# Adding each expert's output rows to token rows in DRAM inside the expert loop, in place of 64 gathers at the end

## The reference

```python
top_scores, top_idx = jax.lax.top_k(masked, K)          # K = 4 experts of 32 for each token
gates = jax.nn.softmax(top_scores, axis=-1)
capacity = max(1, int(N / E * K * CAP_FACTOR))          # 2048 / 32 * 4 * 1.25 = 320
pos = jnp.cumsum(onehot, axis=0)[jnp.arange(N * K), flat_e] - 1
keep = pos < capacity
buf = jnp.zeros((E + 1, capacity, d), xf.dtype).at[e_s, p_s].set(xf[tok])[:E]
h = jax.nn.silu(jnp.einsum('ecd,edh->ech', buf, wg)) * jnp.einsum('ecd,edh->ech', buf, wu)
out_e = jnp.einsum('ech,ehd->ecd', h, wd)
gathered = out_e[flat_e, jnp.minimum(pos, capacity - 1)]
contrib = gathered * (flat_g * keep.astype(xf.dtype))[:, None]
routed = jnp.zeros_like(xf).at[tok].add(contrib)
return (shared + routed).reshape(b, s, d)
```

## Time and profile before

| | |
|---|---|
| median of three runs | 1864.75 us |
| the profiled execution: own time | 1868.67 us |
| the profiled execution: span of its records | 1867.0 us |
| PE busy | 1544.0 us (83%) |
| DVE busy | 1014.4 us (54%) |
| ACT busy | 798.5 us (43%) |
| POOL busy | 887.1 us (48%) |
| mean granted TensorE clock | 0.931 of full speed |
| DMA traffic | 118.25 MB |

### The profile page before, as it was taken

One profiled execution on the slowest core, in us unless ns is written; L12 is line 12 of the kernel. 1 busy time (PEld: TensorE's weight loads), 2 busy tenths in 40 slices (PEclk: granted clock), 3 DMA queues, 4 the chain that ended last, 5 costly groups with the idle time before them and its releaser, 6 DMA issues.

```text
span 1867.0 us, 25548 instructions
## 1 busy us (share of the span) xinstructions
PE 1544.0 (83%) x7946; PEld 1085.8 (58%) x7946; DVE 1014.4 (54%) x1423; ACT 798.5 (43%) x1543; POOL 887.1 (48%) x775
## 2 busy tenths in 40 slices
PE   2799999999999999999999996441999999999800
PEld 2455555655555555455555554331789999999800
DVE  5456556556555565655655555710366666666533
ACT  2345344444444544445444444200256666666500
POOL 4356657666665675766666572175000101101175
PEclk8899999999999999999999997575999999999955
DMA  9000000000000000000000001022055555555237
GB/s 305 13 16 18 1 21 13 0 21 12 7 14 12 12 8 12 12 8 12 12 10 11 12 1 68 1 102 78 8 185 188 173 164 184 172 169 184 69 104 121
DMA packets 82412, 118.25 MB, mean 63 GB/s; under 512 B 7940, under 2 KB 56775, under 8 KB 82375
## 3 DMA queue, kind: packets, MB, share of 16 engines
q1 hardware_dynamic: 72647, 90.52, 15.6%
q0 software_dynamic: 9728, 27.28, 5.3%
HBM read 77.29 MB, written 31.46 MB: 58 GB/s over the span
## 4 chain that ended last, share of the span: by engine, by line
PE 60%; issue 13%; POOL 12%; DVE 7%; ACT 4%; another core or an unknown queue 1%; DMA 1%; POOLq 0%; DVEq 0%; ACTq 0%; SPq 0%
PE ps_o L720 9%; PE ps_t L634 9%; PE ps_m L634 7%; POOL arena L548 7%; PE ps_st L634 7%; PE ps_m L685 6%; PE ps_st L705 4%; PE ps_o L816 4%; PE ps_m L816 4%; PE ps_t L740 3%; PE ps_st L709 3%; POOL arena L598 3%; ACT arena L1301 2%; POOL arena L553 2%; PE ps_t L834 2%
## 5 line engine op out<-in xcount | busy, mean ns | idle before, releaser
L548 POOL TENSOR_TENSOR arena<-arena 128x512 f32<-128x512 f32 (+1 forms) x512 | 655.9, 1282 | 395.8 <-ACT arena L1301 368.3
L1301 ACT ACTIVATE arena<-ps_st 128x512 f32<-128x512 f32 (+1 forms) x576 | 326.0, 595 | 453.4 <-PE ps_st L709 442.0
L1002 DVE TENSOR_REDUCE arena_r<-ps_m 128x1 fp32r<-128x1101 f32 x256 | 332.1, 1297 | 306.1 <-PE ps_m L685 305.8
L705 PE MATMUL ps_st<-arena_r 128*128 128x512 f32 (+1 forms) x576 | 263.0, 457 | 23.1 <-ACT arena L1301 23.0
L720 PE MATMUL ps_o<-arena 128*64 128x512 f32 (+1 forms) x1152 | 268.4, 601 | 0.0
L582 POOL DMA_DIRECT2D y_slots<-arena x32 | 23.2, 726 | 437.1 <-ACT arena L1382 343.8
L709 PE MATMUL ps_st<-arena_r 68*128 68x512 f32 (+2 forms) x576 | 228.8, 397 | 0.9 <-DVE arena_r L1009 0.9
L634 PE MATMUL ps_m<-arena_r 128*128 128x320 f32 (+1 forms) x864 | 162.9, 324 | 68.9 <-issue 44.5
L685 PE MATMUL ps_m<-arena_r 128*128 128x512 f32 (+1 forms) x768 | 193.2, 360 | 5.4 <-DVE arena_r L1002 5.4
L685 PEld LDWEIGHTS ps_m<-arena_r 128*128 128x128 f32 x768 | 137.6, 191 | 91.0 <-issue 44.6
L634 PEld LDWEIGHTS ps_m<-arena_r 128*128 128x128 f32 x864 | 137.2, 191 | 75.9 <-issue 50.8
(11 more groups left out here) (144 smaller groups left out, 1899.8 us busy)
## 6 DMA issues: line engine op xcount, KB each, us to landing
arena<-in_L_ffn_wg_dram SPq DMA_DIRECT2D x32, 512.0 KB, 3.6
arena<-in_L_ffn_wu_dram SPq DMA_DIRECT2D x32, 512.0 KB, 4.7
arena<-in_L_ffn_wd_dram SPq DMA_DIRECT2D x32, 512.0 KB, 6.4
x_slots<-zeros SPq DMA_DIRECT2D x1, 10240.0 KB
arena_r<-arena_r SPq DMA_DIRECT2D x32, 275.2 KB, 3.6
arena<-x_slots SPq DMA_DIRECT2D x32, 256.0 KB, 2.7
y_slots<-arena POOLq DMA_DIRECT2D x32, 256.0 KB, 5.5
x_sb<-in_x_dram SPq DMA_DIRECT2D x2, 1024.0 KB, 7.3
```

What stands on the lines that cost most here:

```text
L548: pool.tensor_tensor(acc, probsT[0:rows, h, 0, :] if kt == 1 else acc, probsT[0:rows, h, kt, :], ALU.add).then_inc(added, 1)
L705: pe.matmul(ps_st[0:rows, n % 2, :], k1[b][h][:, r], q1[h][:, c:c + 512], start=True, stop=False)
L1002: dve.tensor_reduce(neg[h][:, c:c + 1], scores_m[:, 0:KEYS], AX.X, ALU.max, negate=True)\
L1301: act.activation(probsT[0:rows, h, kt, :], ps_st[0:rows, n % 2, :], ACT.Exp)\
```

## The change

A row of the slot table becomes 272 numbers in place of 256. Behind the 256 of the token stand the token's id (`TOK`), its four gates (`GATES`) and its four expert numbers (`IDS`). Before the expert loop SP writes `x_sb`, which then holds x plus attention plus shared part, into a DRAM table `acc_rows`. In each window DVE converts the ids to integers and finds the gate of each slot by comparing the four expert numbers with the number of the current expert (`slot_gates`); ACT multiplies by that gate as it copies the product out; and POOL issues three indirect DMAs that add the rows to `acc_rows` at their ids. Empty slots carry the ids of 320 spare rows behind the tokens, with gate 0. `y_slots`, the 64 gathers and the 64 multiply-adds of DVE are gone, and the output is a copy of `acc_rows`, DRAM to DRAM.

```diff
-    YRING = 8
+    RW = D + 16
+    TOK, GATES, IDS = D, D + 1, D + 1 + TOPK
...
-            sp.dma_start(xslots[0:SLOTS, :].rearrange("(p n) d -> p n d", p=P),
-                         zeros[:, :].unsqueeze(1).broadcast_to([P, SLOTS // P, D])).then_inc(init_out, 16)
+            spare = xslots[0:SLOTS, :].rearrange("(e j p) d -> j p e d", e=E, p=FP)
+            for j in range(FJ):
+                sp.dma_start(acc[NTOK + j * FP:NTOK + (j + 1) * FP, :], fill[:, j, 0:D]).then_inc(init_out, 16)
+                sp.dma_start(spare[j], fill[:, j, :].unsqueeze(1).broadcast_to([FP, E, RW])).then_inc(init_out, 16)
...
+            for c in range(NCHUNK):
+                for i in (2, 3):
+                    job_done(sp, J_SHARED + i, c * 2)
+                sp.dma_start(acc[c * 512:(c + 1) * 512, :].rearrange("(t p) d -> p t d", p=P),
+                             x_sb[:, c * 4:c * 4 + 4, :]).then_inc(acc_in, 16)
             sp.wait_ge(xslots_out, 16 * NT * TOPK)
 
             def feed(par, turn, weights):
                 e = turn * 2 + par
 
                 sp.wait_ge(job_ready[1], (J_EXPERT // 2 - 2 + 1) + e)
+                sp.wait_ge(ids_done, e * 2 + 2)
                 sp.dma_start(xg[par][:, 0:CTL - 1, :],
...
+            sp.wait_ge(add_out, 16 * CTL * E)
             for b in range(B):
-                sp.wait_ge(summed, (b + 1) * QT_N)
-                sp.dma_start(out[b].rearrange("(t p) d -> p t d", p=P), x_sb[:, b * QT_N:(b + 1) * QT_N, :])\
-                  .then_inc(final_out, 16)
+                sp.dma_start(out[b], acc[b * S:(b + 1) * S, :]).then_inc(final_out, 16)
...
+            pool.wait_ge(init_out, 32 * FJ)
             attend(BEFORE, -1)
...
-            def store(par, turn):
+            pool.wait_ge(acc_in, 16 * NCHUNK)
+
+            def add(par, turn):
                 e = turn * 2 + par
                 pool.wait_ge(ysb_ready, e * CTL + CTL + 2)
                 pool.sem_inc(pool_step, 1)
-                pool.dma_start(yslots[bass.ds(e * CAP, (CTL - 1) * P), :].rearrange("(c p) d -> p c d", p=P),
-                               y_sb[par][:, 0:CTL - 1, :]).then_inc(ystore_out, 16)
...
-                pool.wait_ge(ystore_out, e * 32 + 32)
+                for c, (_, rows) in enumerate(CAP_TILES):
+                    pool.indirect_dma_start(
+                        out=acc[:, :], in_=y_sb[par][0:rows, c, :], in_offset=None, compute_op=ALU.add,
+                        out_offset=bass.IndirectOffsetOnAxis(ap=ids[0:rows, par, c:c + 1].bitcast(U32), axis=0))\
+                        .then_inc(add_out, 16)
+                pool.wait_ge(add_out, (e + 1) * 16 * CTL)
                 pool.sem_inc(ysb_free, 1)
...
+            dve.sem_inc(ids_done, 4)
...
+            def slot_gates(par, turn):
+
+                e = turn * 2 + par
+                dve.wait_ge(rows_in[par], turn * 32 + 32)
+                dve.wait_ge(ysb_free, e + 1)
+                dve.tensor_copy(ids[:, par, 0:CTL], xg[par][:, :, TOK]).then_inc(ids_done, 1)
+                dve.scalar_tensor_tensor(picks[:, :, :], xg[par][:, :, IDS:IDS + TOPK], iota_e[:, bass.ds(e, 1)],
+                                         xg[par][:, :, GATES:GATES + TOPK], ALU.is_equal, ALU.mult)\
+                   .then_inc(picked_up, 1)
+                dve.wait_ge(picked_up, e + 1)
+                dve.tensor_reduce(slot_gate[:, par, :], picks[:, :, :], AX.X, ALU.add).then_inc(ids_done, 1)
...
                        (lambda ht: ht < 2 and weights_lo(par, n + ht, ht)) if more else None)
+                slot_gates(par, turn)
                 if more:
                     rows_lo((par + 1) % 2, turn + par)
...
-                    act.activation(y_sb[par][0:rows, c, :], ey_bank[(par * CTL + c) % 2][0:rows, 0:D], ACT.Copy)\
+                    act.activation(y_sb[par][0:rows, c, :], ey_bank[(par * CTL + c) % 2][0:rows, 0:D], ACT.Copy,
+                                   scale=slot_gate[0:rows, par, c:c + 1])\
                        .then_inc(ysb_ready, 1)
...
                 act.wait_ge(ysb_free, turn * 2 + par + 1)
+                act.wait_ge(ids_done, (turn * 2 + par) * 2 + 6)
```

More of the change, by code:

```diff
@@ L191, in xattn_moe @@
     WPIECES = 4
[L193 to L194 removed]
+    xslots = nc.dram_tensor("x_slots", [SLOTS + NTOK * TOPK, RW], F32, kind="Internal").ap()
+    acc = nc.dram_tensor("acc_rows", [NTOK + CAP, D], F32, kind="Internal").ap()
     with ExitStack() as stack:
@@ L254, in xattn_moe @@
         w_raw = [carve(3 * W) for _ in range(2)]
-        xg, y_sb = ([carve(CTL * D, "p (c n) -> p c n", c=CTL) for _ in range(2)] for _ in range(2))
-        carve = carver(arena, 6 * W + NT * D)
+        xg, y_sb = ([carve(CTL * n, "p (c n) -> p c n", c=CTL) for _ in range(2)] for n in (RW, D))
+        carve = carver(arena, 6 * W + NT * RW)
         silu, hid32 = ([carve(512) for _ in range(2)] for _ in range(2))
@@ L280, in xattn_moe @@
         ones = sb("ones", [P, P])
-        zeros = sb("zeros", [P, D])
+        FP = 64
+        FJ = CAP // FP
+        assert FJ * FP == CAP
+        fill = arena[0:FP, R_SUM:R_SUM + FJ * RW].rearrange("p (j d) -> p j d", j=FJ)
         gb = sb("gb", [P, 4, DT])
@@ L328, in xattn_moe @@
         rows_in = [sem(f"rows_in{i}") for i in range(2)]
-        ystore_out = sem("ystore_out")
-        yg_in = [sem(f"yg_in{i}") for i in range(YRING)]
+        acc_in, add_out = sem("acc_in"), sem("add_out")
+        ids_done, picked_up = sem("ids_done"), sem("picked_up")
         copies_in = [sem(f"copies_in{i}") for i in range(B)]
@@ L359, in xattn_moe @@
         hid_hi_done, hid_done = sem("hid_hi_done"), sem("hid_done")
-        ey_ready, ysb_ready, ysb_free, summed = (sem(n) for n in ("ey_ready", "ysb_ready", "ysb_free", "summed"))
+        ey_ready, ysb_ready, ysb_free = (sem(n) for n in ("ey_ready", "ysb_ready", "ysb_free"))
         def job_in(ev, turn, off=0):
@@ L496, in _ @@
             seq = Chain(pool, pool_seq)
-            seq.done(pool.memset(zeros[:, :], 0.0))
+            seq.done(pool.memset(fill[:, :, :], 0.0))
             seq.done(pool.memset(ident[:, :], 0.0))
@@ L508, in _ @@
             seq.done(pool.iota(iota_e[:, :], pattern=[[1, E]], base=0, channel_multiplier=0,
+                               allow_small_or_imprecise_dtypes=True))
+            seq.done(pool.iota(fill[:, :, TOK], pattern=[[FP, FJ]], base=NTOK, channel_multiplier=1,
                                allow_small_or_imprecise_dtypes=True))
@@ L581, in store @@
                 pool.sem_inc(pool_step, 1)
-                pool.dma_start(yslots[bass.ds(e * CAP, (CTL - 1) * P), :].rearrange("(c p) d -> p c d", p=P),
-                               y_sb[par][:, 0:CTL - 1, :]).then_inc(ystore_out, 16)
-                lo, rows = CAP_TILES[-1]
-                pool.dma_start(yslots[bass.ds(e * CAP + lo, rows), :], y_sb[par][0:rows, CTL - 1, :])\
-                    .then_inc(ystore_out, 16)
-                pool.wait_ge(ystore_out, e * 32 + 32)
+                for c, (_, rows) in enumerate(CAP_TILES):
[4 more added lines that the diff above has]
+                pool.wait_ge(add_out, (e + 1) * 16 * CTL)
                 pool.sem_inc(ysb_free, 1)
             with pool.Fori(0, E // 2) as i:
[L591 to L601, removed]
+                add(0, i)
+                add(1, i)
         @block.tensor
@@ L1143, in _ @@
             seq.done(dve.tensor_scalar(keep[:, :, :], posk[:, :, :], float(CAP), None, ALU.is_lt))
+            seq.done(dve.tensor_copy(h_row[:, :, IDS:IDS + TOPK], topf[:, :, :]))
+            seq.done(dve.tensor_scalar(h_row[:, :, TOK], dropslot[:, :, 0], -float(SLOTS), 1.0 / TOPK, ALU.add, ALU.mult))
+            seq.wait()
             seq.done(dve.tensor_scalar(topf[:, :, :], topf[:, :, :], float(CAP), None, ALU.mult))
@@ L1154, in _ @@
             seq.wait()
[L1155 to L1158, removed]
+            seq.done(dve.tensor_copy(h_row[:, :, GATES:GATES + TOPK], gate[:, :, :]))
             seq.wait()
@@ L1214, in _ @@
             expert(1, E // 2 - 1, False)
[L1216 to L1222, removed]
         @block.scalar
```

18 lines of the change are left out of this document (10 added, 8 removed).

## The result

The changed kernel takes 1902.89 us (median of 4 runs, 1899.92 to 1905.66) against 1866.12 for the kernel before (4 runs, 1864.67 to 1868.23): 1.0196 times as long, 95% interval 1.0176 to 1.0216, so 36.8 us slower. The profiled execution took 1899.92 us with a span of 1898.0, which is 31.0 us more span than before. (The profiled executions are the fastest of the changed kernel and the slowest of the kernel before, so they lie closer together than the medians.)

A forecast was written before the change was run, and what follows sets the result against it. PE was taken to bound the expert loop, at 12.83 us per expert. Entry 2.1 plus loop 131.1 minus tail 78.6 gave +54.6 us, so 1864.75 became 1919 us, range 1860 to 1990.

The forecast's parts named there:

- The deciding step: Expert loop: SP's new wait for slot_gates(e-2) holds back the weight loads, making a longer loop; 131.1 us more over 30 windows.
- 1. gates to first weight issue: Expert loop, SP: release, two row loads and registers between the end of slot_gates and the first weight issue; 1.4 us.
- 2. issue to last landing: Expert loop, weight DMA: first weight issue to last landing, with the adds running beside it; 7.8 us, bounds 6.8 and 8.8.
- 3. landing to gates, full clock: Expert loop: from landed weights through ACT, DVE and PE's fourth stripe to the end of slot_gates; 7.2 us.
- 4. clock: Expert loop, PE: idling about 3 us per window lowers the clock for the fourth stripe; 0.8 us, between none and 1.9.
- period: Expert loop: time per expert as the sum of four steps, 17.2 us (bounds 15.4 and 19.3) against 12.83.
- The tail: After the last product: 97.3 us replaced by POOL's start, adds, landing and output copy, 18.7 us; 78.6 us saved.
- "Nothing" for the fill: Kernel start: larger fill from 64 partitions ends near 58 us, before the first score matmul at 67.75, so costs nothing.
- the x store: Loop entry: SP stores the last x_sb chunk before loading the first rows, delaying PE's start by 1.5 us, bounds 0 and 5.
- The saved tail wins: Rival: period under 15.38 us makes the kernel faster; 1841 us at 14.6 us per expert, 1788 at best; chance 0.10.
- POOL is not the bound: Rival, expert loop: slow adds make POOL the bound; at 21 us per expert 2034 us; chance 0.07.
- Engines that stall in each burst of adds: Rival, expert loop: each burst of three indirect DMAs holds ACT 3.6 us; period 20.8 us, time 2028 us; chance 0.06.

The follow-up runs named there:

- Experiments 1, 2 and 4: 1: changed kernel, weight loads ahead of SP's wait, 1798.61 us; 2: changed kernel, slot_gates at window's start, 1799.48 us; 4: kernel before plus the wait alone, 1923.6 us.
- no_adds: Changed kernel without POOL's three indirect adds and their wait, experts' outputs missing from the result: 1894.21 us, ratio 1.0133.
- order_only: Changed kernel with the weight loads issued ahead of the two row loads, but still behind SP's wait for ids_done: 1845.67 us, ratio 0.9871.
- weights_first: Changed kernel with SP issuing the three weight loads before it waits for ids_done and loads the rows: 1798.61 us, ratio 0.9619.
- wf_both: weights_first with the fill sent from 128 partitions and expert 0's row loads ahead of the last x store: 1792.06 us, ratio 0.9593.

## Why the prediction was right

**The deciding step** held as it was written: gates, SP, weight DMA, ACT, DVE, PE, gates. Experiments 1, 2 and 4 show it from three sides. Term by term:

| | forecast | measured |
|---|---|---|
| 1. gates to first weight issue | 1.4 | 1.51 |
| 2. issue to last landing | 7.8 | 7.32 (6.63 to 8.31) |
| 3. landing to gates, full clock | 7.2 | 6.82 |
| 4. clock | 0.8 | 0.82 |
| period | 17.2 | 16.43 |

Steps 2 and 3 were each set 0.4 to 0.5 too long, and 30 x 0.77 = 23 us are nearly all of the distance between the forecast 54.6 and the 30.7 that the profiled executions differ by. (The medians differ by 36.8.) ACT's wait for the weights was forecast at 3 to 4 us in each window and is 2.7 on average (78.5 over 29); PE's idle time was set at 3 us and is 2.1. In step 2 I had put the adds beside the landing as a cost; without any adds it is 7.26 (no_adds), so they cost nothing that shows there. The Trainium skill (DMA: Bandwidth & Descriptors, Rules for kernel authors) says that an accumulate reads its destination and writes it later. If that doubled traffic were felt, it would be in the period, and the runs show none of it there: 16.43 with and 16.46 without.

**Step 4** was a guess between 0 and 1.9, and that 0.8 came out at 0.82 is luck. In single windows it is anything from 0 to 1.55 us. That a wait shorter by a microsecond makes it vanish, so that 14.6 and 16.6 us per expert lie 0.9 us of delay apart, was not foreseen.

**The tail** was forecast at 18.7 us and took 16.3. The landing of the last add was 1.8 us and not 4; the issues were slower than assumed (1.86 us apart and not 1.29); the copy was 8.6 us where 10.5 were taken.

**The entry and the start.** This is the part that failed. "Nothing" for the fill rested on 250 GB/s, a peak of other copies; it flowed at about 203, and its last part landed at 50.67 + 20.5 = 71.2 us and not at 58. The Trainium skill's rule (SBUF — State Buffer, Door 1: The DMA port swizzle) by which 64 partitions reach half of the ports was the better one. The estimate from its figures was 218 GB/s and an end near 65 us; the trace has 7% less rate and an end 6 us later. The 0 to 2 us taken from it were short of the 4.7 us by which the scatters begin late (0.6 were forecast). Only 1.1 of these are left when PE ends the shared part (1353.27 in place of 1352.21). From there to expert 0 it is 8.2 us in place of 5.6, and this 2.6 is the x store, forecast at 1.5. Together 3.7 us, where 2.1 were forecast.

**Rivals.** "The saved tail wins" needed a period under 15.38 us. order_only reached 14.37 and is indeed faster than the kernel before, by 1.3% (ratio 0.9871), so the break-even point was placed well. POOL is not the bound: it waits 420.2 us for ACT. Engines that stall in each burst of adds: in weights_first PE is busy 98% of the loop with all the adds in it.

## What to carry to other kernels

- Where an in-order queue gets a new wait, list everything behind it. A prefetch that does not need what is waited for goes ahead of the wait, or the releasing instructions go to the earliest place where their inputs are there: either was worth 104 us here.
- A delay that lets TensorE idle a little longer in every turn of a loop isn't priced by its own length. Here 0.85 us of delay cost 2.0 us per turn, of which 1.0 came with the lower clock; read the granted clock of the whole loop, not of one window.
- A fill or a store that starts from 64 partitions is checked against the DMA rate of one from 128 before its end is called hidden.

## What was not expected of the hardware

- The clock in the loop: PE's wait of 1.2 us per window left it at 1.00, with one of 2.1 us it was 0.89 over the loop, and 17 of 27 windows show it.
- The indirect add costs POOL 1.56 us for 128 rows of 1 KB and the plain scatter 0.97, while the DMA traffic of the adds beside the weights cost the loop nothing that shows (DMA busy share 0.64 with them, 0.54 without adding).
- A source on 64 partitions brought the fill's rate down to 203 GB/s, against 352 from 128, with the same bytes.
- While 64 scatters are issued, the other engines nearly stop (PE is busy for 4.6 of 60 us from 1240 to 1300 in wf_both), and their waits lead back to "remote" or "issue", for which the profile names no engine of the core. In the kernel before it is the same. At most two in flight gave 20 us back; a limit of four never took hold. In the expert loop bursts of three do no harm. The cause was not found.
